# Gathered rows turned by transposing transfers and joined on GpSimd, with the routing steps and first loads placed anew

## The reference

```python
x = x + layernorm(attention(layernorm(x), Wq, Wk, Wv, Wo, b_out))   # 32 heads of 8, 8 kv heads, rope, causal
x = x + layernorm(ffn(layernorm(x), ...))

def ffn(x):                                   # E, TOPK, H, I, NSH = 8, 2, 256, 640, 2
    scores = sigmoid(x @ w_router.T)          # 2048 x 8
    topk_w, topk_i = top_k(scores, 2); topk_w /= sum(topk_w)
    out = sum over a token's 2 experts e of topk_w * wd[e] @ (silu(wg[e] @ x) * (wu[e] @ x))
    return out + sum over j in 0, 1 of sd[j] @ (silu(sg[j] @ x) * (su[j] @ x))
```

## Time and profile before

| | us |
|---|---|
| median of 3 runs (lowest, highest) | 668.69 (666.15, 670.47) |
| the profiled execution | 663.51 |
| its span, first to last instruction | 661.7 |
| PE, PEld, DVE, ACT, POOL busy in it | 635.1, 515.2, 529.9, 419.6, 320.4 |

### The profile page before, as it was taken

One profiled execution on the slowest core, in us unless ns is written; L12 is line 12 of the kernel. 1 busy time (PEld: TensorE's weight loads), 2 busy tenths in 40 slices (PEclk: granted clock), 3 DMA queues, 4 the chain that ended last, 5 costly groups with the idle time before them and its releaser, 6 DMA issues.

```text
span 661.7 us, 15279 instructions
## 1 busy us (share of the span) xinstructions
PE 635.1 (96%) x5914; PEld 515.2 (78%) x5914; DVE 529.9 (80%) x1055; ACT 419.6 (63%) x786; POOL 320.4 (48%) x516
## 2 busy tenths in 40 slices
PE   8988899999999979999999999999999999999995
PEld 6844455555656547888889999999999999888884
DVE  5789999999988744479868888888887888558886
ACT  2526788888887885542247777787877787522222
POOL 3225557767766761100274454545454430078853
PEclk9988999999999999999999999999999999999998
DMA  3853633645540000000366786877776864032311
GB/s 97 171 129 71 109 83 67 131 100 154 101 96 15 19 10 17 17 0 1 120 226 233 245 282 231 252 248 242 248 273 223 262 230 152 25 88 84 100 49 63
DMA packets 79670, 87.09 MB, mean 132 GB/s; under 512 B 54352, under 2 KB 69072, under 8 KB 79600
## 3 DMA queue, kind: packets, MB, share of 16 engines
q0 software_dynamic: 11872, 54.53, 25.1%
q1 hardware_dynamic: 67312, 31.08, 19.5%
q10 hardware_dynamic: 416, 0.52, 0.3%
HBM read 63.83 MB, written 9.31 MB: 111 GB/s over the span
## 4 chain that ended last, share of the span: by engine, by line
PE 76%; DVE 11%; issue 3%; ACT 3%; SPq 2%; POOL 2%; DMA 1%; another core or an unknown queue 0%; POOLq 0%; DVEq 0%; ACTq 0%
PE PS L547 72%; DVE NM L1052 3%; DVE NM L1048 2%; PE PS L558 2%; PE PS L754 1%; ACT PF L901 1%; SPq L1564 1%; POOL PF L1470 1%; SPq L1570 1%; DMA XG<-xn,XIDX 1%; DVE X L1317 1%; PE PS L702 1%; DVE RR L1013 1%; DVE WL L1336 1%; DMA X<-in_x 1%
## 5 line engine op out<-in xcount | busy, mean ns | idle before, releaser
L1257 DVE TENSOR_TENSOR HF<-SS,PS 128x256 f32<-128x256 f32 (+2 forms) x141 | 68.7, 487 | 71.2 <-PE PS L547 34.3
L1336 DVE TENSOR_TENSOR WL<-RAW,WH 128x768 fp32r<-128x768 f32 x125 | 118.5, 959 | 4.4 <-ACT WH L856 4.1
L947 ACT ACTIVATE SS<-PS 128x256 f32<-128x256 f32 (+2 forms) x141 | 62.0, 439 | 80.2 <-PE PS L547 66.5
L1470 POOL TENSOR_SCALAR_AFFINE_SELECT PF<-PF 128x512 f32<-128x512 f32 x128 | 83.4, 676 | 57.4 <-ACT PF L901 56.8
L856 ACT ACTIVATE HH<-HF 128x256 fp32r<-128x256 f32 (+1 forms) x120 | 58.0, 483 | 73.2 <-DVE HF L1257 65.6
L547 PE MATMUL PS<-WH,HH 128*128 128x256 f32 x355 | 103.3, 291 | 0.6 <-DVE HL L1350 0.3
L901 ACT ACTIVATE PF<-PS 128x1536 f32<-128x1536 f32 x64 | 92.9, 1452 | 17.1 <-PE PS L547 15.5
L856 ACT ACTIVATE WH<-RAW 128x768 fp32r<-128x768 f32 x125 | 103.3, 841 | 0.0
L547 PE MATMUL PS<-WL,HH 128*128 128x256 f32 x355 | 100.3, 282 | 0.0
L547 PE MATMUL PS<-WH,HL 128*128 128x256 f32 x355 | 100.2, 282 | 0.0
L547 PE MATMUL PS<-XGL,WH 128*128 128x256 f32 x320 | 90.5, 283 | 0.0
(11 more groups left out here) (206 smaller groups left out, 1467.2 us busy)
## 6 DMA issues: line engine op xcount, KB each, us to landing
ys<-YO SPq DMA_DIRECT2D x16, 256.0 KB
RAW<-in_wsh SPq DMA_DIRECT2D x4, 768.0 KB, 5.0
XT<-in_xt SPq DMA_DIRECT2D x8, 256.0 KB, 3.3
X<-in_x SPq DMA_DIRECT2D x8, 256.0 KB, 3.5
xn<-YY SPq DMA_DIRECT2D x16, 128.0 KB, 1.7
out<-X SPq DMA_DIRECT2D x15, 128.0 KB
ys<-YO SPq DMA_DIRECT2D x7, 128.0 KB
RAW<-in_wsh SPq DMA_DIRECT2D x2, 384.0 KB, 4.6
```

The costliest lines, as they stand in the source:

```text
L947: eng.activation(ss, both(i, bank(b))[0], ACT.Silu).then_inc(free[b] if dense(i) else silu, 1)
L1257: eng.tensor_tensor(hf, ss, both(c, bank(b))[1], ALU.mult).then_inc(free[b], 1)
L1336: eng.tensor_tensor(WL[q % 2][:, c], RAW[raw_of(q)][:, c], WH[q % 2][:, c].bitcast(F32), ALU.subtract).then_inc(w_lo, 1)
L1470: eng.affine_select(out=o, in_=o, pattern=[[0, 4], [1, 128]], base=0, channel_multiplier=-1, compare_op=ALU.is_ge, fill=0.0).then_inc(zero ...
```

## The change

1. XN2 holds each row as 256 low 16-bit halves and 256 high ones instead of 256 fp32 values. POOL makes that form (YH, a strided copy of 512 16-bit elements, in stage `b_norm2`, for 16 tiles), and SP's store waits for it; ACT's next write of YY waits for POOL's copy instead of the store.
2. Rows are gathered as 16-bit halves. SP turns them by one transposing transfer per unit (`across`: 128 x 1024 halves for a wide unit, 128 x 512 for a narrow one) into XT16. POOL joins the halves into fp32 columns X32 by two strided copies (stage `join`, in the first chunk of the unit before; 512 elements per partition each for a wide unit, 256 for a narrow one). ACT rounds X32 to XGH, DVE forms XGL in the place of X32, with both inputs now in SBUF. The 78 transposes on PE are gone. Rows are gathered a unit further ahead.
3. The routing steps lie in other chunks: `rank` ahead of `up(10)`, `token` behind `up(15)`, and the tables PICK, CHOOSE and TAILS accordingly.
4. SP's loads of x for sequence 3 and the constants (now six transfers, the identity apart) are issued behind the first two transfers of maxima into QT instead of ahead of the queries' transposing transfer.

```diff
-TAILS = (3, 2, 1, 2, 2, 3, 1, 1, 3, 3, 1, 2, 1, 3)
-RANK, TOKEN, ROWS0 = 11, 17, 19.0
-PICK = {3: [(0, 0)], 4: [(0, 1)], 5: [(0, 2), (0, 3), (0, 4)], 6: [(0, 5), (0, 6)], 7: [(0, 7), (0, 8)], 8: [(0, 9), (1, 0), (1,
-        1)], 9: [(1, 2), (1, 3), (1, 4), (1, 5), (1, 6), (1, 7), (1, 8), (1, 9)]}
-CHOOSE = {9: [0], 10: [1, 2, 3, 4, 5, 6, 7, 8], 12: [9, 10, 11, 12], 13: [13, 14], 14: [15], 15: [16, 17, 18, 19],
-          17: [20, 21], 18: [22]}
+TAILS = (3, 2, 1, 2, 2, 3, 1, 0, 3, 3, 0, 2, 3, 3)
+RANK, TOKEN, ROWS0 = 10, 15, 19.0
+PICK = {2: [(0, 0)], 4: [(0, 1)], 5: [(0, 2), (0, 3), (0, 4)], 6: [(0, 5), (0, 6)], 7: [(0, 7)], 8: [(0, 8), (0, 9),
+        (1, 0), (1, 1), (1, 2), (1, 3), (1, 4), (1, 5), (1, 6), (1, 7), (1, 8), (1, 9)]}
+CHOOSE = {9: [0, 1, 2, 3, 4, 5, 6, 7, 8], 10: [9, 10], 11: [11, 12, 13], 12: [14], 13: [15, 16, 17, 18, 19], 15:
+        [20], 17: [21], 19: [22]}
...
+        if DENSE <= c < LAST and CHUNKS[c][1] == 0 and sequence(c) < NK:
+            out.append(("join", sequence(c)))
+        if c + 1 == ROWS0:
+            out.append(("join", 0))
...
-                read(e, ("xt", q - 1))
+                e.wait_ge(x_lo, q)
...
-            def turn_block(k):
-                n = UNITS[k][1]
-                e.wait_ge(d_xg[k % 2], gathered(k))
-                c = take(("xt", k))
-                for q in range(n):
-                    for h in range(2):
-                        at = 128 * n * h + 128 * q
-                        t = eng.transpose(bank(c, at, at + 128), XG[:, k % 2, q, 128 * h:128 * h + 128], identf)
-                t.then_inc(full[c], 1)
...
                     made(e, ("b_turn2", i - 2))
-                    e.wait_ge(d_xn[i % 2], 16 * (i // 2))
+                    e.wait_ge(y_16, i - 1)
...
                 elif what == "xt":
-                    made(e, s)
+                    n = 256 * UNITS[i][1]
+                    e.wait_ge(x_32, 2 * i + 2)
                     if i >= 2:
-                        e.wait_ge(dn, first_of(i))
-                    n = 256 * UNITS[i][1]
-                    copy(XGH[:, i % 2, 0:n], bank(c, 0, n)).then_inc(x_hi, 1)
+                        made(e, ("up", first_of(i) - 1))
+                    copy(XGH[:, i % 2, 0:n], X32[:, i % 2, 0:n]).then_inc(x_hi, 1)
...
-                    eng.tensor_tensor(XGL[:, i % 2, 0:n], bank(c, 0, n), XGH[:, i % 2, 0:n].bitcast(F32), ALU.subtract).then_inc(free[c], 1)
+                    eng.tensor_tensor(XGL[:, i % 2, 0:n], X32[:, i % 2, 0:n], XGH[:, i % 2, 0:n].bitcast(F32), ALU.subtract).then_inc(x_lo, 1)
...
                 if k >= 2:
-                    made(e, ("xt", k - 2))
+                    e.wait_ge(d_t[k % 2], 16 * (k // 2))
...
-                elif what == "xt" and i < NK - 2:
-                    block_rows(i + 2)
+                elif what == "join":
+                    q = UNITS[i][1]
+                    e.wait_ge(d_t[i % 2], 16 * (i // 2 + 1))
+                    if i >= 2:
+                        made(e, ("up", first_of(i) - 1))
+                    x = X32[:, i % 2, 0:256 * q].bitcast(U16).rearrange("p (k q t h) -> p h k q t", k=2, q=q, h=2)
+                    for h in range(2):
+                        eng.tensor_copy(x[:, h], XT16[i % 2][:, 0:q, h, :, :].rearrange("p q k t -> p k q t")).then_inc(x_32, 1)
+                elif what == "xt":
+                    for k in (2, 3) if i == 0 else (i + 3,) if i < NK - 3 else ():
+                        block_rows(k)
+                elif what == "b_norm2":
+                    e.wait_ge(c_x2, i + 1)
+                    e.wait_ge(d_xn[i % 2], 16 * (i // 2))
+                    eng.tensor_copy(YH[:, i % 2, :, :], YY[:, i % 2, :].bitcast(U16).rearrange("p (c h) -> p h c", h=2)).then_inc(y_16, 1)
...
+            def across(k):
+                n = UNITS[k][1]
+                e.wait_ge(x_32, 2 * (k - 1))
+                e.wait_ge(d_xg[k % 2], gathered(k))
+                eng.dma_start_transpose(XT16[k % 2][:, 0:n, :, :, :].rearrange("p q h k t -> p (q h k) t"),
+                                        XG[:, k % 2, 0:n, :].rearrange("p q c -> p (q c)")).then_inc(d_t[k % 2], 16)
...
-                    if T and b < NB - 2:
+                    if T and b < NB - 2 and b != 1:
                         load_xt(b + 2)
                         load_x(b + 2)
-                    if i == 3:
-                        constants()
...
+                    if i == 0:
+                        load_xt(3)
+                        load_x(3)
+                        constants()
...
                 elif what == "b_norm2":
-                    e.wait_ge(c_x2, i + 1)
-                    eng.dma_start(XN2[128 * i:128 * i + 128, :], YY[:, i % 2, :]).then_inc(d_xn[i % 2], 16)
+                    e.wait_ge(y_16, i + 1)
+                    eng.dma_start(XN2[128 * i:128 * i + 128, :], YH[:, i % 2, :, :].rearrange("p h c -> p (h c)")).then_inc(d_xn[i % 2], 16)
+                elif s == ("choose", 20):
+                    across(0)
+                    across(1)
+                elif what == "xt" and i < NK - 2:
+                    across(i + 2)
```

More of the change, by code:

```diff
@@ L8 @@
 BF16 = mybir.dt.bfloat16
+U16 = mybir.dt.uint16
 U32 = mybir.dt.uint32
@@ L287, in banks @@
             use[s] = (b, count[b])
-        elif s[0] in ("rank", "token", "xt", "cross"):
+        elif s[0] in ("rank", "token", "cross"):
             b = 6 + crossed % 2
@@ L337, in build @@
         mhalf = sb("mhalf", [P, 1], F32)
-        CF = sb("CF", [P, 512], F32)
-        identf = CF[:, 0:128]
-        LT = CF[:, 128:192]
-        iota = CF[:, 192:320]
-        pcol = CF[:, 320:321]
-        tvec = CF[:, 321:353]
-        LT256 = CF[:, 361:425]
-        k256 = CF[:, 425:441]
-        units = CF[:, 441:441 + 2 * NK]
-        CR = sb("CR", [P, 256], BF16)
-        ES = sb("ES", [P, NT, NE], F32)
+        identf = sb("IDF", [P, 128], F32)[:, :]
+        tables = ExitStack()
+        CF = sb("CF", [P, 384], F32, tables)
+        LT = CF[:, 0:64]
+        iota = CF[:, 64:192]
+        pcol = CF[:, 192:193]
+        tvec = CF[:, 193:225]
+        LT256 = CF[:, 233:297]
+        k256 = CF[:, 297:313]
+        units = CF[:, 313:313 + 2 * NK]
+        CR = sb("CR", [P, 256], BF16, tables)
+        ES = sb("ES", [P, NT, NE], F32, tables)
+        tables.close()
+        XT16 = [sb("XT16a", [P, 2, 2, 2, 128], U16)]
+        sb("rest2", [P, 128], F32)
         CMB = sb("CMB", [P, NT, NE], F32)
@@ L416, in build @@
         WL.append(sb("WL1", [P, 3840], F32R))
-        SG = sb("SG", [P, 3, 128], F32)
-        SM = sb("SM", [P, 2, 16], F32)
-        SELB = sb("SELB", [P, NT, NE], BF16)
-        CNT = sb("CNT", [P, 8], F32)
-        C64 = sb("C64", [P, 2, 8, 8], F32)
+        ranking = ExitStack()
+        SG = sb("SG", [P, 3, 128], F32, ranking)
+        SM = sb("SM", [P, 2, 16], F32, ranking)
+        SELB = sb("SELB", [P, NT, NE], BF16, ranking)
+        CNT = sb("CNT", [P, 8], F32, ranking)
+        C64 = sb("C64", [P, 2, 8, 8], F32, ranking)
+        ranking.close()
+        XT16.append(sb("XT16b", [P, 2, 2, 2, 128], U16))
+        sb("rest3", [P, 104], F32)
         NBK = sb("NBK", [P, 2, 8], F32)
@@ L439, in build @@
         WIDX = sb("WIDX", [P, NK], U32)
-        XG = sb("XG", [P, 2, 2, 256], F32)
+        halves = ExitStack()
+        YH = sb("YH", [P, 2, 2, 256], U16, halves)
+        halves.close()
+        XG = sb("XG", [P, 2, 2, 512], U16)
         XGH = sb("XGH", [P, 2, 512], F32R)
+        whole = ExitStack()
+        X32 = sb("X32", [P, 2, 512], F32, whole)
+        whole.close()
         XGL = sb("XGL", [P, 2, 512], F32R)
         YO = sb("YO", [P, 2, 2, 256], F32)
-        XN2 = nc.dram_tensor("xn2", (NT * P, 256), F32, kind="Internal").ap()
+        XN2 = nc.dram_tensor("xn2", (NT * P, 512), U16, kind="Internal").ap()
         YS = nc.dram_tensor("ys", (SUB * P, 256), F32, kind="Internal").ap()
@@ L474, in build @@
         right0, top0, laid, n_m, scored, expd, pv, sums, zeroed, ev = (sem(n) for n in ("right0", "top0", "laid", "n_m", "scored", "expd", "pv", "sums", "zeroed", "ev"))
+        y_16, x_32, x_lo = (sem(n) for n in ("y_16", "x_32", "x_lo"))
+        d_t = [sem(f"d_t{k}") for k in range(2)]
         wrs, w_hi, w_lo, h_hi, h_lo, dn, rt, x_hi, ymix = (
@@ L800, in _ @@
                     e.wait_ge(ev, i + 1)
-                    e.wait_ge(d_cf, 16)
+                    e.wait_ge(d_cf, 32)
                     half_turn(s, YC[:, i % 2, :], identf)
@@ L846, in _ @@
                     tokens()
-                elif what == "xt":
-                    turn_block(i)
         @block.scalar
@@ L863, in _ @@
                 made_by = {"f_taken": "f_qkv", "turned": "turn",
-                           "b_turned": "b_turn", "b_taken": "b_out", "b_high": "b_turn2", "b_kept": "b_route", "xt": "xt"}.get(what)
+                           "b_turned": "b_turn", "b_taken": "b_out", "b_high": "b_turn2", "b_kept": "b_route"}.get(what)
                 if made_by:
@@ L1545, in constants @@
```

(3 more changed lines are left out.)

1 line of the change is left out of this document (removed).

## The result

The changed kernel is not faster. Its 20 runs have a median of 677.49 us (667.69 to 695.42); the kernel before, run in turn with it 20 times, has 668.79 us (665.34 to 672.33). The ratio of the comparison is 1.0059, 95% interval 1.0037 to 1.0081. That ratio rests on the runs near each kernel's fastest, so it leaves out the longer half of the changed kernel's runs, and this spread is part of the effect: the medians alone stand at 1.013. On a second chip the unchanged copy gave 1.0209.

The account below looks back on a forecast made before the run. PE was taken as the bound from about 250 to 650 us. The terms -8.5 - 0.8 + 0.8 + 0.5 + 0 + 0.5 - 1.9 gave -9.4 us, a median of 659.3 us, range 654 to 671.

Parts of the forecast that it names:

- Parts 1, 2, 3, 6 and 7: Transposes off PE -8.5, first rows -0.8, moved routing +0.8, YH copy in attention +0.5, first loads -1.9 us.
- Part 1: All units: the 78 transposes leave PE, which was taken as the bound there, -8.5 us.
- YH's copy: Attention: 16 copies of 512 elements on POOL, 0.7 us each, +0.5 us in all, ends 0 and 3.
- Part 7: Front: first loads moved, maxima's transfers go 2.6 us earlier, PE's wait for them goes, -1.9 us, ends -2.6 and 0.
- Parts 2 and 3: PE's wait for unit 0's first rows goes, -0.8 us; routing steps moved to other chunks, +0.8, ends 0 and 2.5.
- the place that was feared: Moved routing steps where DVE has 14.88 of 16 us busy; rival: too dense, +4.5, 664, chance 0.12.
- Part 4: Routed units: POOL's joins and DVE stop each other, mostly within DVE's idle time, +0.5 us, ends 0 and 6.
- part 2: Unit 0: its rows' longer way ends at 337 to 338, wanted at about 341, so PE's wait goes, -0.8 us.
- XGH waiting for the join: Routed units: ACT's highs held up by POOL's joins, listed as a sign of being wrong, without a size.
- only the narrow units and those with two WL per chunk feel it: Rival, joins holding DVE in those units: half the routed part's gain goes, +4.5, 664 us, chance 0.14.
- The slower rival: Wide units: joins hold DVE until it becomes the bound; 681 us at 1.4 us per copy, chance 0.09.
- Part 5: Routed units: transposing transfers raise DMA share from 0.76 to about 0.88; weights 0, upper end 3; SP's late stores 0.

Follow-up runs that it names:

- neither: The changed kernel without transposing transfers, join copies cut to 4 of 128 columns, routed rows wrong: 653.9 us, 0.9856 of the kernel before; repeated 653.19 us, 0.9853.
- pe_turns_moved: The kernel before with only the change's routing tables and order of first loads, rows still turned by PE: 661.12 us, 0.9963 of the kernel before.
- front_only: The kernel before with only the first loads moved behind the first transfers of the maxima: 661.36 us, 0.9978 of the kernel before.
- idle_across: `neither` plus 23 transposing transfers of the changed kernel's sizes that only SP waits for: 653.49 us, 0.9853 of the kernel before; one of four runs 670.74.
- idle_again: `idle_across` repeated unchanged, 9 runs: 661.18 us in the median (653.06 to 669.11), 0.9908 of the kernel before.
- rows_at_join: The changed kernel with POOL's gather for the unit after next issued right behind the joins: 666.04 us in the median (662.29 to 687.64), 1.0013 of the kernel before.
- after_again: The changed kernel, unchanged, run again on one of the experiments' chips: 681.45 us in the median of six, 1.0209 of the kernel before.
- rows_first: `rows_at_join` with POOL's gather issued ahead of the two join copies instead of behind them: 677.39 us (676.15 to 679.1), 1.0224 of the kernel before.
- the two single executions: One of 2753 us, of a kernel without transposing transfers and with a unit's two joins in successive chunks; one of 1974 us, of `after_again`; in no ratio.

## Why the prediction was wrong

659.3 us was predicted, with 654 to 671; the median is 677.5. Five of the seven parts came out within 0.5 us in their sum; the other two terms, both about what stands beside PE, were far too small.

- **Parts 1, 2, 3, 6 and 7** sum to -9.9 us in the prediction. `neither`, which holds these and the shortened joins, measured -9.4 and -9.8. Part 1 alone: from `pe_turns_moved` to `neither` the units take 223.4 and 215.3 us, -8.1 for the -8.5. YH's copy measured 612 ns for the 0.7 us. Part 7: -1.5 for -1.9, with PE's wait at 44.97 gone as said. Parts 2 and 3 were put at 0 together, and unit 0 starts at 340.50 in `front_only`, at 340.31 in the changed kernel and at 341.50 in `neither`, so they are 0 within 1 us; PE was busy in 15.87 of the 16 us from 300 to 316, the place that was feared.
- **Part 4, first failed step: "+0.5 for all 23 units; the ends are 0 and 6".** Measured +7.5. The price of a copy was nearly right (0.78 us in the median of the joins of the first buffer, stops included; 0.7 taken). What failed was the cover: the slack of 1.7 us per unit and the wait of 0.46 us before HF were read from one wide unit with wide ones on both sides, and spread over all. In the wide units ahead of narrow ones two chunks hold two WL each and DVE has no slack in them; they have most of the wide units' 3.4 us. In the narrow units DVE has slack, but the way from the joins over XGH and XGL to the next unit's first matmul is 1.0 us longer than in `neither` and had 0.5 to give; that is 4.3 us. The prediction has this way for unit 0 alone (part 2) and gives it no term in part 4, though it names "XGH waiting for the join" as a sign of being wrong. The rival "only the narrow units and those with two WL per chunk feel it" names both places, with 5 us for the joins where the runs show 7.5; by which way the narrow units feel it is not in it. The slower rival, DVE as the bound of every wide unit, is not what happened.
- **Part 5, second failed step: "Weights have a unit's lead, so 0" and "SP now waits ... nobody near: 0".** The load was put at 25 us of the 16 queues. q1's share went from 20.2% of 652.0 us in `neither` to 26.7% of 651.8 in `idle_across`, 42 us, and the DMA share of the wide stretch from 0.74 to 0.89 and more, to 1.05 in the long run. The fast runs of `idle_across` and `idle_again` show that this load alone can cost nothing. What the working passed over is the wait that the change adds on POOL: `block_rows` there now waits for a transposing transfer, and behind it in POOL's queue stand weights and joins. 3 us or so are left of the transfers when that wait is moved (`rows_at_join`); with it the changed kernel lies another 0.5% to 2% higher. For SP's order, "nobody near" fails as well: in `idle_again` a store to `ys` went 7.5 us late behind a transposing transfer and PE waited 2.44 us in the end.
- **The range.** 671 would have held a sum with the upper ends of parts 4 and 5 (-9.4 + 5.5 + 3 gives 667.8 on the median), but the POOL wait was no case at all.

What stays open: why some landings take 9 to 17 us. The medians are alike, 5.3 us in the long run of `after_again`, 5.4 in `idle_across` and 5.7 in `idle_again`; it is a few transfers that differ from run to run. The DMA share of the wide stretch was 1.05 and 0.98 in the profiles of `after_again` and `idle_again`, which have late ones, and 0.89 and 0.81 in those of `idle_across` and `rows_first`, which have none over 10 us; that a lower share prevents them was not tested. Longer runs have lower granted clocks (0.977 to 0.991 in those of the changed kernel above 677 us, 0.996 in the fastest), and in the long profile PE's clock was 0.97 over a stretch in which PE was often idle; that may be a consequence of the waiting and was not tested as a cause.

## What to carry to other kernels

Read slack at the tightest place that the new work will meet, not at a typical one: here work that fits in an ordinary wide unit, with 1.7 us to spare, cost 7.5 us in and around the narrow ones. Read it for every way to the bounding engine, too: an engine's idle time did not help where the new step stood on a chain of four engines with half a microsecond to give. A new wait on an engine's queue costs what is queued behind it, so put it where that engine waits for the same event already. And try the unglamorous parts of a change alone: `pe_turns_moved`, 0.9963 of the kernel before, is the fastest of this study among those that give the reference's results, with `front_only` within the noise of it.

## What was unexpected in the hardware

- Two strided 16-bit copies of POOL and a DVE instruction with two SBUF inputs stop each other. Mostly each is stopped once: a WL of 0.96 us takes 1.46, and the two copies 2.40 instead of 1.46 together. Once both copies ran first, and the WL took 2.56. The Trainium skill, page SBUF — State Buffer, section Who interferes with whom, says that DVE and GpSimd share a port pair under an exclusive lock, and that the one that comes second is fully blocked. The lengths fit full stops; in the row at 457.24, though, the WL is on record 0.34 us ahead of the first copy, so the order in which they came is not shown by it. ACT's copies of the same 512 elements (774 ns) left WL at 960 ns.
- 23 transposing transfers of 0.13 or 0.26 MB from SBUF to SBUF took 42 us of all 16 queues, 0.12 MB per busy us, beside gathers; in the attention, at 59% share, it was 0.2.
- With them in flight, single landings can be late, differently from run to run: 4.3 to 17.4 us for their own in one profile and 3.3 to 8.1 in another, 11.58 us for a plain store of 3.2. The kernels without them spread by 0.3 to 7 us, with them by 11 to 38 in all but `rows_first`, where it is 3 (the two single executions left out).
